# Cross-attention on one core: the add that completes the rotated queries moves within VectorE's slot

## What is computed

```python
h = rmsnorm(x, norm_w)
q = rope(h @ Wq.T);  k, v = split(ctx @ Wkv.T);  k = rope(k)
scores = einsum('bqhd,bkhd->bhqk', q, k) / sqrt(32)
out = softmax(scores) @ v            # heads side by side, 512 features
return x + out @ Wo.T
```

## Time and profile before

| | us |
|---|---|
| median of 3 runs (1513.32 to 1514.33) | 1513.55 |
| the profiled execution | 1510.65 |
| its span, first to last instruction | 1508.9 |
| setup, up to the first query projection | 210 |
| slot 16 (starts at 353.14) to the end of the loop and drain | 1156 |
| TensorE busy | 1342.6 |
| VectorE busy | 1285.7 |
| ScalarE busy | 955.9 |
| GpSimd busy | 869.0 |

### The profile page before, as it was taken

How to read it: one execution, slowest core, us unless ns; L and a number is a source line. 1 busy time by engine, 2 the same in 40 slices (tenths; PEclk the granted TensorE clock), 3 DMA queues, 4 the chain that set the end, 5 groups by cost and what they waited for, 6 DMA issues and landing times.

```text
span 1508.9 us, 35021 instructions
## 1 busy us (share of the span) xinstructions
PE 1342.6 (89%) x12104; PEld 767.3 (51%) x12104; DVE 1285.7 (85%) x1696; ACT 955.9 (63%) x1330; POOL 869.0 (58%) x738
## 2 busy tenths in 40 slices
PE   2887777899999999999999999999999999999987
PEld 1443343455555555555555555555555555555544
DVE  3755567899999999999999999999999999999984
ACT  2623346677667776677766777676777667776652
POOL 1324456666666566665666656666666666665552
PEclk9998898999999999999999999999999999999999
DMA  3423244455545454555555554545555555453442
GB/s 129 150 94 103 93 100 97 105 131 138 135 137 136 119 131 117 133 136 131 136 133 138 138 138 124 132 117 133 136 131 136 131 136 137 118 131 92 112 124 84
DMA packets 171564, 187.53 MB, mean 124 GB/s; under 512 B 91152, under 2 KB 145552, under 8 KB 163312
## 3 DMA queue, kind: packets, MB, share of 16 engines
q1 hardware_dynamic: 168720, 181.70, 45.8%
q10 hardware_dynamic: 2784, 5.05, 0.9%
HBM read 92.16 MB, written 43.65 MB: 90 GB/s over the span
## 4 chain that ended last, share of the span: by engine, by line
ACT 28%; PE 25%; DVE 17%; issue 15%; ACTq 1%; DVEq 1%
DVE q_rot L1112 13%; PE a_ps L927 11%; ACT p_part L1056 10%; ACT probs L1042 10%; PE b_ps L1002 4%; PE score_ps L912 3%; ACT h_t L169 3%; ACT o_part L1051 3%; ACT junk L134 2%; DVE h_t L175 1%; PE b_ps L940 1%; ACT v_part L1062 1%; PE a_ps L1002 1%; PE score_ps L954 1%; ACTq L74 1%
## 5 line engine op out<-in xcount | busy, mean ns | idle before, releaser
L1095 POOL TENSOR_TENSOR p_part<-probs,p_part 77x1536 f16<-77x1536 f32 x128 | 396.1, 3095 | 35.2 <-ACT p_part L1056 25.3
L927 PE MATMUL a_ps<-h_t,wq 128*128 128x512 f16 x1536 | 384.8, 404 | 6.8 <-PEq L232 3.1
L1002 PE MATMUL b_ps<-wo,o_part 128*128 128x512 f16 x1464 | 338.3, 381 | 0.0
L1083 POOL TENSOR_TENSOR q_part<-q_rot,q_part 128x512 f16<-128x512 f32 x128 | 148.3, 1158 | 207.4 <-ACT q_part L1036 207.4
L1112 DVE TENSOR_TENSOR q_rot<-cos_part,sin_part 128x512 f32<-128x512 f32 x128 | 265.6, 2075 | 0.8 <-POOL sin_part L1091 0.8
L927 PEld LDWEIGHTS a_ps<-h_t,wq 128*128 128x128 f16 x1536 | 158.0, 103 | 211.9 <-issue 52.2
L1042 ACT ACTIVATE probs<-score_ps,scales 77x2048 f32<-77x2048 f32 x128 | 250.1, 1954 | 8.8 <-PE score_ps L912 7.6
L1056 ACT ACTIVATE p_part<-probs 77x2048 f16<-77x2048 f32 x128 | 243.6, 1903 | 0.0
L1002 PEld LDWEIGHTS b_ps<-wo,o_part 128*128 128x128 f16 x1464 | 143.5, 98 | 147.6 <-issue 3.2
L1091 POOL TENSOR_TENSOR sin_part<-swapped,consts 128x512 f32<-128x512 f32 x128 | 163.6, 1278 | 65.4 <-DVE swapped L1153 65.4
L1164 DVE TENSOR_REDUCE maxima<-score_ps 128x16 f16<-128x1232 f32 x128 | 183.2, 1431 | 1.9 <-PE score_ps L954 1.9
(11 more groups left out here) (118 smaller groups left out, 2068.4 us busy)
## 6 DMA issues: line engine op xcount, KB each, us to landing
q_stack<-q_part SPq DMA_DIRECT2D x756, 64.0 KB, 2.1
x_in<-x SPq DMA_DIRECT2D x32, 1024.0 KB, 6.7
res<-x SPq DMA_DIRECT2D x32, 1024.0 KB, 5.9
out<-res SPq DMA_DIRECT2D x64, 512.0 KB, 3.5
v_sb<-v_dram SPq DMA_DIRECT2D x32, 154.0 KB
k_stack<-k_hi_dram SPq DMA_DIRECT2D x64, 77.0 KB, 7.1
c_nat<-ctx SPq DMA_DIRECT2D x19, 256.0 KB, 2.8
v_dram<-v_row ACTq DMA_DIRECT2D x19, 256.0 KB, 2.1
```

The source lines that it names most:

```text
L927: mm = nc.tensor.matmul(a_ps[:, :], wq[:, w, k, g * P:(g + 1) * P], h_t[:, t.parity, h, k, :], start=(k == 0 and w == 0 and h == 0), stop= ...
L1002: mm = nc.tensor.matmul(projection_bank(t, 0)[:, :], o_part[:, par, o, k, j * P:(j + 1) * P], wo[:, w, k, :], start=(k == 0 and o == 0 and ...
L1095: nc.gpsimd.tensor_tensor(p_part[:, g % 2, 1, LO_V:J, :], probs[:, g % 2, LO_V:J, :], p_part[:, g % 2, 0, LO_V:J, :], ALU.subtract).then_i ...
```

## The change

VectorE's add q_rot is taken from the top of the slot, where it served unit s-1, to the place between the low part of o and the row maxima, where it serves unit s. Its waits move with it: for sin_part of this slot (made by GpSimd from what VectorE has just shuffled) and for the low part of q of the unit before. Nothing else is touched; the number of instructions is the same.

```diff
--- before.py
+++ after.py
@@ -1105,12 +1105,6 @@
             def slot(t):
                 i, s, g = t.i, t.s, t.g
 
-                if t.has(1):
-                    dve.wait_ge(q_sin, s)
-                    dve.wait_ge(q_read, s)
-                    wait_from_first(dve, q_lo, s - 1)
-                    nc.vector.tensor_tensor(q_rot[:, :], cos_part[:, :], sin_part[:, :], ALU.add).then_inc(q_full, 1)
-
                 def output():
 
                     if t.has(10):
@@ -1157,6 +1151,12 @@
                     dve.wait_ge(o_hi, s - 5)
                     nc.vector.tensor_tensor(o_part[:, par, 1, h, :], b_ps[:, :], o_part[:, par, 0, h, :],
                                             ALU.subtract).then_inc(o_lo, 1)
+
+                if t.has(0):
+                    dve.wait_ge(q_sin, s + 1)
+                    dve.wait_ge(q_read, s + 1)
+                    wait_from_first(dve, q_lo, s)
+                    nc.vector.tensor_tensor(q_rot[:, :], cos_part[:, :], sin_part[:, :], ALU.add).then_inc(q_full, 1)
 
                 if t.has(1):
                     dve.wait_ge(max_mm, s)
```

## The result

The changed kernel takes 1583.41 us (median of 4 runs, 1576.23 to 1588.71), the kernel before 1513.43 (1511.6 to 1514.33): ratio 1.0461, 95% interval 1.0415 to 1.0506. The forecast was 1564 with a range of 1535 to 1588. So the sign and the main mechanism came as forecast, and the time lies 19 us above it.

What follows compares the result with a forecast made beforehand. TensorE was taken as the bound outside v_part slots, where it waits for L175. Loop +17.8, ramp +14.1, clock +13.5 in the loop and +5 in the ramp: +50.4 us on 1513.55, so 1564 us, range 1535 to 1588.

Steps and rivals of the forecast that it cites:

- The chain and the ordinary slot: Loop slots without v_part: L927, cos_part, shuffle, sin_part, q_rot, maxima, L175, L1017 in sequence; the slot takes 9.29 us.
- The cover of 1.08 us: Ordinary slot before L1017: L175 ends at 6.83 us after L927, TensorE arrives at 7.91; 1.37 added, some 0.3 shows.
- v_part slot: Every fourth loop slot: still waits for p_part, L1017 at 10.37 us after L927, slot 11.42, before 11.46; no gain.
- Who is first: Shared SBUF ports: in the loop q_rot starts 0.15 us before p_part; in slots 4 and 5 GpSimd is first.
- Rival 1: Every slot: GpSimd's p_part is first, q_rot ends at 9.11, ordinary slots take 12.2 us; about 1830 us, chance 0.07.
- The clock in the loop: Behind v_part slots: TensorE idles 2.5 us instead of 2.16, so 8 more slow L927 in 27 batches, +13.5 us.
- L912 follows by 0.15: End of each slot on TensorE: L912 starts 0.15 us after L1017, the next L927 0.89 later.
- The ramp: Slots 0 to 15: +14.1 us from less cover and a locked q_rot, +5 from three more slow L927.
- Setup: Before slot 0: forecast difference 0 us.
- all falls: High end of the range: a clock fall in each of the 27 loop batches, +3.5 us over the forecast.
- five lost races: High end of the range: q_rot comes second to p_part five times, 3 us each, 15 us.

Runs made afterwards that it cites:

- the version with both moved: Changed kernel with v_part's low part also moved, from slots with g = 2 to ahead of cos_part in slots with g = 3: 1472.47 us, ratio 0.975 to before.

## Why the prediction came out as it did

**The chain and the ordinary slot: right, and shown.** 9.28 us against 9.29, each start within 0.02 us. That the move makes the loss follows from undoing it by parts (44.3 us of loop, 26.1 of ramp), and that sin_part's lateness is the cause of the longer slots from the 0.19 us a slot that came back when VectorE made it.

**The cover of 1.08 us: right.** Where v_part and the port are out of the way, TensorE's own slot is 8.96, and the chain adds 0.32.

**v_part slot: right but for the clock.** L1017 comes 10.39 us after L927 (10.37), and the slot is 11.43 (11.42) where the clock stays up till L927. The prediction had every fall come in L927; in 18 of 27 it now comes in L912, inside the v_part slot.

**Who is first: right.** q_rot is locked in slots 4 and 5 (3.56 us each) and once in the drain (slot 127, 3.60), never in the loop. Rival 1 was priced at 1830, and the kernel with q_rot behind the maxima takes 1813; that the two are so near is chance. The built kernel has slots of 11.04 and not 12.2, and 115 us of clock in its loop that the rival did not count.

**The clock in the loop: right in size.** +13.6 against +13.5 us; 23 slow L927 of 27 batches, where 25 were named and 16 were there before. Each fall costs about what it did, 1.8 us against 1.7; 7 more of them came where 8 were counted. The share was a guess between two ends, and that it came so near is partly luck.

**The step that failed: "L912 follows by 0.15".** The prediction took that distance from slots in which TensorE never stood at L1017. Where it does stand there, in a slot with g = 3, L912 comes 0.22 us later still, and 0.6 at the end of the loop body: +10.7 us, the largest part of the 24.7 by which the traces miss the forecast. In the kernel before TensorE waited at L1017 only with g = 2, where this does not show. What is shown is the place (it moves with the end of the body, shrinks where the loop is left, and is absent when L1017 does not wait), that 0.08 us of it is the wait for the keys, and that a body of four batches is loaded anew at its end. That TensorE's sequencer (its instruction stream, which can run ahead of the matmuls), stopped at L1017, reaches the instructions of the loop's end only then, when it had run ahead before, fits this and is argued, not shown.

**The ramp: mechanism right, size too low** (+26.1 against 14.1 + 5). The clock costs 19.0 us there against 10.8 before (counted as above): +8.2, where 5 was counted. By slots, against before: slots 1 to 3 +9.9 (forecast 6.4, and the 5 for the clock); slot 4 +5.9 (5.0); slot 5 +3.7, where 1 was counted: its wait in front of the exp did not hide the lock, since the lock now stands in the chain to L1017, which came at 12.09 instead of 8.40. Slots 6 to 15 +5.0 (1.7), and slot 0 +1.6 by a slow L927 that the prediction had not counted. L927 is slow in slots 0, 2 to 9 and 15 now, before in 4, 6, 7 and 11.

**Setup: no effect of the change is seen.** Slot 0 starts 2.3 us later here, but over the kernels of this study, whose setup is the same, it starts between 209.0 and 212.8 us, and between 209.6 and 212.8 with q_rot moved throughout.

**The range: held, and partly by luck.** Its high end, 1588, was made of all falls, 5 us more of ramp and five lost races. No race was lost in the loop and four batches have no fall; the distance to L912, which the range did not have, took that room.

What stays open: which instructions between L1017 and L912 take the rest of the 0.22 and the 0.6 us.

## What to carry to other kernels

An instruction that shows three times its length because it waits for a port is free as long as nothing behind it is late; here it was nearly so. Before an add is moved next to its producer, write down the chain that the consumer's queue then stands in, and compare it with the bound of the slot: 1.37 us added on 1.08 us of cover gave the ordinary slot to 0.01 us. It did not give the whole loss of the loop: of 44.3 us the clock has 13.6 and the loop's end and the wait for the keys 10.7. And where a bounding engine gets a wait that it had not, count what its sequencer had done in the shade of the work, loop ends above all.

## Of the hardware, not expected

- The end of a loop body of two batches costs TensorE nothing while it is behind its work, and 0.6 us when it waits right in front of it. With a body twice as long, and such a wait, it is 4.3 us, and the granted clock falls to 0.53 behind it.
- The instructions of the body of two batches are loaded once (no packet of an instruction queue between 450 and 1260 us in the version with both moved), those of the body of four in every pass (104 packets between 450 and 1290).
- Waits of 0.24 us in every slot cause no slow L927 (none of 108), the 2.38 us in every fourth slot cause 23 of 27.
- Of two instructions on VectorE and GpSimd that both read two tensors in SBUF, a small lead was enough, 0.14 us for VectorE and 0.07 for GpSimd (slots 4 and 5): the first kept its length, and the second lasted until after it, q_rot 3.45 to 3.56 us instead of 0.69, or p_part 3.49 instead of 3.09.
